# Where and when the frequency mixing's matrices are loaded: in its own stage, or during the tokens' first transform step

## The reference

```python
Vf = jnp.fft.rfft(phi, n=n, axis=0)                 # 16 filters
Uf_p = jnp.fft.rfft(u, n=n, axis=1)                 # the normalised tokens
Uf_m = jnp.fft.rfft(u * sgn3, n=n, axis=1)
U_plus = jnp.fft.irfft(Vf[None, :, :, None] * Uf_p[:, :, None, :], n=n, axis=1)[:, :sl]
U_minus = jnp.fft.irfft(Vf[None, :, :, None] * Uf_m[:, :, None, :], n=n, axis=1)[:, :sl]
...
out = jnp.einsum('btkd,k,kde->bte', U_plus, s, Mpp)
out = out + jnp.einsum('btkd,k,kde->bte', U_minus, s, Mpm)
```

## Time and profile before

| | us |
|---|---|
| three timed runs | 2849.27, 2830.85, 2848.44 |
| their median | 2848.44 |
| the profiled execution | 2834.71 |
| its span in the trace | 2832.9 |
| TensorE busy | 2358.3 (83%) |
| VectorE busy | 1495.8 (53%) |
| ScalarE busy | 1309.7 (46%) |
| GpSimd busy | 366.5 (13%) |
| mean granted clock of TensorE | 0.907 |

### The profile page before, as it was taken

One profiled execution on the slowest core, in us unless ns is written; L12 is line 12 of the kernel. 1 busy time (PEld: TensorE's weight loads), 2 busy tenths in 40 slices (PEclk: granted clock), 3 DMA queues, 4 the chain that ended last, 5 costly groups with the idle time before them and its releaser, 6 DMA issues. The chain is left out here.

```text
span 2832.9 us, 78733 instructions
## 1 busy us (share of the span) xinstructions
PE 2358.3 (83%) x34528; PEld 1799.9 (64%) x34528; DVE 1495.8 (53%) x3482; ACT 1309.7 (46%) x2623; POOL 366.5 (13%) x651
## 2 busy tenths in 40 slices
PE   3549898768169999999999999999785984799898
PEld 2328898633058888888888888888433751344444
DVE  3852433357136665666566566656211452576777
ACT  3443433356046655665566565656210563333332
POOL 1311111124300000000000000000021001122211
PEclk7676977879689999999999999999897886899999
DMA  6457535365621111111101111110398410000000
GB/s 196 144 138 162 107 82 102 73 216 177 153 77 45 45 45 45 45 45 45 36 23 44 45 45 45 45 23 19 123 298 290 140 55 13 13 20 25 21 24 26
DMA packets 155227, 235.09 MB, mean 83 GB/s; under 512 B 18310, under 2 KB 112623, under 8 KB 151372
## 3 DMA queue, kind: packets, MB, share of 16 engines
q1 hardware_dynamic: 122392, 134.74, 16.4%
q0 software_dynamic: 32496, 95.33, 12.5%
HBM read 141.68 MB, written 88.31 MB: 81 GB/s over the span
## 5 line engine op out<-in xcount | busy, mean ns | idle before, releaser
L1026 DVE COPY spc_g<-spc_pz 128x512 f32<-128x512 f32 x1024 | 629.1, 682 | 306.5 <-PE spc_pz L922 306.5
L996 ACT ACTIVATE spc_g<-spc_pz 128x512 f32<-128x512 f32 x1024 | 549.2, 612 | 284.5 <-PE spc_pz L922 284.1
L922 PE MATMUL spc_pz<-spc_v,spc_as 108*128 108x128 bf16 x8192 | 553.9, 219 | 13.8 <-issue 1.7
L922 PEld LDWEIGHTS spc_pz<-spc_v,spc_as 108*128 108x128 bf16 x8192 | 473.6, 97 | 102.7 <-ACT spc_g L996 31.4
L943 PE MATMUL spc_pz<-spc_g,spc_u 128*20 128x128 f32 x16384 | 469.2, 274 | 21.4 <-DVE spc_g L1026 17.3
L943 PEld LDWEIGHTS spc_pz<-spc_g,spc_u 128*20 128x20 f32 x16384 | 451.4, 134 | 47.5 <-ACT spc_g L996 30.1
L1533 PE MATMUL moe_ex<-moe_ew,moe_d 128*128 128x512 f32 x512 | 249.8, 611 | 32.8 <-DVE moe_yt L1690 32.4
L907 PE MATMUL spc_pu<-spc_f,spc_s 128*128 128x256 f32 x768 | 207.6, 396 | 80.6 <-DMA spc_s<-s_sf 80.6
L1690 DVE SCALAR_TENSOR_TENSOR moe_yt<-moe_ex,moe_gb,moe_yt 128x128 f32<-128x128 f32 x768 | 209.6, 343 | 103.3 <-ACT moe_yt L1592 98.0
L566 DVE SCALAR_TENSOR_TENSOR inv_xo<-inv_pa,inv_mask,inv_xo 128x256 f32<-128x256 f32 x256 | 123.6, 484 | 219.7 <-PE inv_pa L524 187.0
L544 ACT ACTIVATE inv_b<-inv_pb 112x1024 f32<-112x1024 f32 x128 | 125.5, 1021 | 216.8 <-PE inv_pb L503 216.8
(11 more groups left out here) (218 smaller groups left out, 2282.0 us busy)
## 6 DMA issues: line engine op xcount, KB each, us to landing
s_yd<-spc_yo SPq DMA_DIRECT2D x128, 160.0 KB
s_sf<-fwd_so SPq DMA_DIRECT2D x16, 1024.0 KB, 6.4
spc_s<-s_sf POOLq DMA_DIRECT2D x32, 512.0 KB, 6.1
ivs_y<-s_yd POOLq DMA_DIRECT2D x32, 512.0 KB, 5.1
s_td<-ivs_to SPq DMA_DIRECT2D x32, 512.0 KB, 5.3
ln_t<-s_td SPq DMA_DIRECT2D x32, 512.0 KB, 3.9
lnc_xc<-in_x SPq DMA_DIRECT2D x32, 256.0 KB, 5.3
s_xn<-lnc_xn SPq DMA_DIRECT2D x64, 128.0 KB
```

Of the source, the lines that this page charges most:

```text
L922: m = pe.matmul(pz[:, (p + 2) % 3, e // 4, 2 * FT * (e % 4):2 * FT * (e % 4) + 2 * FT], AS[:, x, 8 * p + e, :], V[:, k, x, :, FT * t:FT * ...
L996: act.activation(g_out(p, 0), g_in(p, 0), ACT.Copy).then_inc(ga, 1)
L1026: v.tensor_copy(g_out(p, 1), g_in(p, 1)).then_inc(gd, 1)
```

## The change

AS becomes a buffer of a new function `second_mixer`, which calls `forward` and `spectrum` within its life. Its twelve loads leave POOL's queue and the start of `spectrum`. ScalarE issues them in `forward`, for n = 1 to 6 one behind `normalise(n + 1, 1)` and one behind `normalise(n + 1, 3)`, load i = 2n - 2 + c // 2. ScalarE waits for all of them before it leaves `forward`. TensorE's wait for `as_in` in `spectrum` goes. The transfers themselves have the same sources, sizes and destinations within the buffer.

```diff
-def forward(nc, I, S):
+def forward(nc, I, S, AS):
...
+        as_in = A.sem("as_in")
...
+            def mixers(i):
+                g, x = divmod(i, 2)
+                act.dma_start(AS[KX * g:KX * g + KX, x].rearrange("k e d -> k (e d)"),
+                              S["AS"][x, A_PARTS[g]].rearrange("k e d -> k (e d)")).then_inc(as_in, 16)
...
                     if n + 1 < NU:
                         normalise(n + 1, c)
+                    if 1 <= n < 7 and c % 2:
+                        mixers(2 * n - 2 + c // 2)
                 if n + 2 < NU:
                     deviation(n + 2)
+            act.wait_ge(as_in, 16 * 12)
...
-def spectrum(nc, I, S):
+def spectrum(nc, I, S, AS):
...
-        AS = A.sb("as", [KROWS, 2, C, C], BF16)
...
-        as_in = A.sem("as_in")
...
-            for g, part in enumerate(A_PARTS):
-                for x in range(2):
-                    sp.dma_start(AS[KX * g:KX * g + KX, x].rearrange("k e d -> k (e d)"),
-                                 S["AS"][x, part].rearrange("k e d -> k (e d)")).then_inc(as_in, 16)
-
...
-            pe.wait_ge(as_in, 16 * 12)
...
+def second_mixer(nc, I, S):
+
+    with Arena(nc, "mats") as A:
+        AS = A.sb("as", [KROWS, 2, C, C], BF16)
+        forward(nc, I, S, AS)
+        spectrum(nc, I, S, AS)
...
-STAGES = (first_mixer, forward, spectrum, inverse, layer_one)
+STAGES = (first_mixer, second_mixer, inverse, layer_one)
```

## The result

| us | before | after |
|---|---|---|
| median of five timed runs | 2848.44 | 2795.56 |
| lowest and highest | 2830.85, 2851.43 | 2790.38, 2821.14 |
| the profiled execution | 2834.71 | 2806.48 |
| its span | 2832.9 | 2804.7 |
| `forward` (its first memset to POOL's first issue in `spectrum`) | 168.0 | 186.0 |

The ratio of the two kernels' times on record is 0.9864, with a 95% interval of 0.9827 to 0.9901: 28 to 49 us less. So the kernel is faster, by 1.0 to 1.7%; that it is faster by over 1% is likely, but not shown. With five runs each, which spread by 21 and 31 us, the figure depends on how it is taken: the medians lie 52.9 us apart (ratio 0.9814), the means 42.2. The forecast was 2818 (range 2788 to 2850), 22 us too high. The changed program has its lines 1 to 3 further down.

The account below looks back on a forecast made before the run. Bounds: tokens queued behind 7.1 MB of AS loads in `spectrum`, and `forward`'s loop waiting for a small table. Terms -58.7 + 30.0 + 6.4 = -22.3 us, from a mean of 2840.8 to 2818; own range 2803 to 2829, wider range 2788 to 2850.

Parts of the forecast that it names:

- rival A: In `forward`, AS loads interleave well, costing 2.7 us each: 16 + 6.4 added, 36 saved, 2805 us; chance 0.18.
- The queue ahead of the tokens: At the start of `spectrum`, tokens no longer stand behind 7.1 MB: L907 starts after 7.5 us, 58.7 us less (55 to 60).
- The covers named for V(0) and the second tokens: In `spectrum`, V(0) follows 2.1 us behind the first table; tokens of f = 1 have 12 us of L907 matmuls as cover.
- ScalarE's issues and the end wait at nothing: In `forward`, twelve DMA issues, 5 to 6 us in sum, and the wait at the end cost 0.
- for c = 3: In `forward`, six loads issued amid the stores each delay an even filter's table by 5.0 us: 30.0 us more.
- For c = 1: In `forward`, these loads go out when the DMA engines are idle and the filters under way: 0 us.
- For the clock: In `forward`, longer waits make the granted clock fall four more times, 1.6 us each: 6.4 us more.
- The step that failed: In `forward`, the c = 3 load is issued when normalise ends, at 644.7, amid the stores and ahead of the table.
- The sign that was to be looked for: In `forward`, the six even waits for `fwd_fw` from f = 4 on are 6 to 7 us.
- B: In `forward`, both loads of a period fall ahead of the table: 61.4 us more, 2843 us; chance 0.25.
- C: In `forward`, the clock stays down at 1.2 GHz: 81 us more, less 58.7, 2864 us; chance 0.08.
- D: At the start of `spectrum`, the tokens are slow by themselves; only 36 us of cost stay, 2877 us; chance 0.04.

Follow-up runs that it names:

- small loads: Changed kernel, each of the twelve AS loads cut to the first 8 of 128 rows e (2 KB of 32 KB): forward 168.1 us, ratio 0.9802.
- c = 3 alone: Changed kernel with only the six loads at c = 3 whole, the other six cut to 8 rows e: forward 177.8 us.
- the second run: The changed kernel run once more unaltered, beside the version before it: forward 185.2 us, ratio 0.9852.
- the loads placed best: Changed kernel with eight AS loads of 36 and 18 rows, all in idle windows, the 36-row ones first: forward 171.7 us, ratio 0.9805.
- c = 1 alone: Changed kernel with only the six loads at c = 1 whole, the other six cut to 8 rows e: forward 170.1 us.

## Why the prediction came out as it did

- **The number: inside the range, and partly by luck.** The median, 2795.6, lies in 2788 to 2850 because the range takes in rival A as counted from the shortest of the timed runs before (2831 less 43). It is outside the forecast's own 2803 to 2829, and the saving, 38.7 us by the ratio and 40.6 by the stages, is above its 12 to 38. What follows is why.
- **The queue ahead of the tokens: right.** 7.5 us to L907 and 58.7 saved were predicted; 7.63 and 58.6 were measured, 7.6 to 8.6 in every kernel with the tokens first. The covers named for V(0) and the second tokens held.
- **ScalarE's issues and the end wait at nothing: right.** The small loads show it (168.1 us); an issue is 0.27 to 0.55 us, and POOL's wait at the border stays at 9.97.
- **The mechanism in `forward`: right; its size: wrong.** The bytes hold up the table in a loop that waits for it, but the stage grew by 18.0 us, not 36.4. Three terms: for c = 3, 6 x 5.0 = 30; alone it measured 9.7 of the stage's length. For c = 1, nothing; alone it measured 2.0. For the clock, 6.4; the filters' excess over 1.90 us adds up to 6.7 us in five of them, before to 3.9 in three, so 2.8 more, and that is already in what the runs above measured (the mean granted clock in the stage is 0.84, before 0.85). The remaining 6.3 is mostly f = 4 meeting both loads, and is in none of them.
- **The step that failed** is "The c = 3 load is issued when normalise ends, at 643.05 + 1.64 = 644.7, in the middle of that crowd". ScalarE's queue did not wait for the activations in front of it where no semaphore said so: the load went out 2.4 us before that end, ahead of the stores. In the changed kernel a c = 3 load goes out at 656.91 and the stores at 657.37; just behind, a window shows the engines at about the share of AS alone (0.57) and well below the 1.03 they reach when the stores are on them. The c = 1 load, too, goes out earlier: the prediction has it 2.8 us behind the start of filters(6) (653.3 against 650.54), and in the changed kernel it goes out 2.8 us ahead of it (664.05 against 666.83), with the table of f = 6 still under way; alone it costs little even so (2.0 us for six). The window of the c = 3 load:

```profile
658.00:660.00 2.00, 1.27 (x6) 0.44 (x4) 1.97 (x6) 1.36 (x4) 0.35 (x1) 1.00 0.63 134
```

 The Trainium skill, *Perfetto Trace Analysis*, section *Per-instruction lifecycle*, says as much: a sequencer pushes an activation into a wait queue and decodes the next instruction. The prediction did not use it. Made to wait for the end of normalise, four of the same six loads do cost 4.8 to 5.9 us, the price the prediction gave them, and two cost nothing. Forward is then 190.6 against 168.1 us, 22.4 more, where the prediction's two terms make 36.4. So its main error was the moment, and the second that it charged every round alike.
- **The sign that was to be looked for**, six even waits of 6 to 7 us, didn't show: they were 11.3, 2.8, 3.8, 1.3, 0.2 and 1.7, and odd filters waited too (0.5, 3.5, 4.9). The stretch from filters(2) to (14), for which it gave 134 us (A 120, B 159), was 116.0.
- **The rivals.** A gave 2.7 us a load and 36 saved; measured were 2.4 a landing for c = 3 alone and 40.6 saved: by size this is the case that came. Its reason was idle time of the engines; what the runs show is that the price hangs on the moment of issue. B came once, at f = 4 (11.30 us of waiting, as it said 11 to 12), and again there in the second run (12.04). C is refuted by the clock above, D by the 7.63 us.
- **The median.** Forecast 2818, measured 2795.6: 18.4 of the 22.4 us are the term above (36.4 less 18.0), the other 4 are within what separates one set of runs from the next.

## What to carry to other kernels

A stage that begins with a long load of constants can gain nearly the whole load if an earlier stage has idle DMA time, and little from a better order within its own queue (58.8 against 4.9 us up to G). What the earlier stage loses comes off again: 18.0 us here, 3.7 with the loads placed best. Before the loads are placed, ask at what moment the queue really issues them, and which small transfer on the critical loop is in flight then: a load of the same size cost about nothing in idle windows (97.3 us for the loop against 97.5), 2.4 us ahead of the loop's stores, and 5 to 6 behind them when it came close to the table. The tail of such a schedule needs cover as much as its loop does.

## What was not expected of the hardware

- ScalarE's DMA issues run ahead of unfinished activations, as shown above.
- 36 rows load at 151 GB/s, 18 rows at 118. The Trainium skill, *SBUF — State Buffer*, section *Door 1: The DMA port swizzle*, gives eight ports, about 218 GB/s, for partitions 0 to 63, where half of these loads lie; the measurement is well below that.
- A large part of the spread between runs arises in `first_mixer`, which is the same in all kernels: `forward` starts between 552.2 us (the changed kernel again) and 585.0 us (c = 1 alone), while `forward` without AS bytes repeats within 0.3 us (168.0, 168.1, 168.3). The windows of 270 to 400 us, first of the changed kernel, then of its second run:

```profile
270.00:400.00 130.00, 118.65 (x2152) 111.97 (x2153) 42.58 (x88) 44.92 (x46) 18.60 (x32) 0.74 0.46 87
```
```profile
270.00:400.00 130.00, 117.32 (x2695) 110.37 (x2692) 54.18 (x112) 55.68 (x58) 22.68 (x39) 0.96 0.54 105
```

 With TensorE as busy in both, the granted clock is 0.74 in one and 0.96 in the other, and 2152 against 2695 matmuls are done. What decides it no run here shows. Lengths of stages, not whole times, told these kernels apart.
